# Vision tower, first routing: sets of constant products on TensorE, and three banks for the weights' turns

## The reference

```python
pooled = x.reshape(B, C, 14, 16, 14, 16).sum(axis=(3, 5))      # 16 x 16 patches
h = einsum('bcij,ce->bije', pooled, channel_weights)            # 196 tokens of 192
h = h + attention(layernorm(h), Wq, bq, Wk, bk, Wv, bv)         # one head of 192
# mixture of nested experts on y = layernorm(h)
logits = einsum('bnc,ec->bne', y, w_router); probs = softmax(logits)
gate, idx = top_k(swapaxes(probs, 1, 2), 98)                    # 98 of 196 tokens for each of 4 experts
hidden = w1 on the chosen tokens, the first 24, 48, 96 or 192 features by expert
x_mlp, q, k, v = split(hidden)                                  # 768 and 3 x 192
x_attn = attention with 12 heads of 16 over q, k, v
out = w2 on concat(gelu(x_mlp), x_attn), again by expert, weighted with the gates
h = h + y + both halves of out
```

## Time and profile before

| | us |
|---|---|
| median of 3 runs | 1766.48 |
| lowest, highest | 1763.33, 1769.15 |
| the profiled execution's own time | 1757.22 |
| its span in the profile | 1755.4 |
| TensorE busy | 1517.8 (86%) |
| VectorE busy | 1218.5 (69%) |
| ScalarE busy | 847.3 (48%) |
| mean granted clock of TensorE | 0.939 |

### The profile page before, as it was taken

The page is one execution under the profiler, slowest core; times in us unless marked ns, Lnnn a source line. Parts: engine busy times, 40 slices in busy tenths (PEclk is TensorE's granted clock), DMA queues, the critical chain, the costliest instruction groups (busy, mean ns, idle before and its releaser), DMA issues.

```text
span 1755.4 us, 34644 instructions
## 1 busy us (share of the span) xinstructions
PE 1517.8 (86%) x12440; PEld 1258.9 (72%) x12440; DVE 1218.5 (69%) x2824; ACT 847.3 (48%) x1934; POOL 248.9 (14%) x319
## 2 busy tenths in 40 slices
PE   2146889898998999988998899989899989999998
PEld 2033778687786878777786777778687778878786
DVE  6658678757887578766887488765787677563552
ACT  0002555455554465454554555545554555546653
POOL 3021012200211002200111002300022002110000
PEclk9986889889999899998999899999899999989999
DMA  8985665516662475615673366706655152102220
GB/s 228 241 205 159 164 159 149 144 42 159 170 184 60 110 180 150 163 34 144 162 181 95 86 161 171 187 15 158 145 151 145 38 147 51 35 19 60 50 53 15
DMA packets 99574, 218.02 MB, mean 124 GB/s; under 512 B 61359, under 2 KB 75853, under 8 KB 88654
## 3 DMA queue, kind: packets, MB, share of 16 engines
q10 hardware_dynamic: 12032, 150.94, 32.4%
q1 hardware_dynamic: 87374, 64.88, 16.4%
HBM read 186.57 MB, written 28.90 MB: 123 GB/s over the span
## 4 chain that ended last, share of the span: by engine, by line
PE 50%; DVE 24%; issue 13%; DMA 7%; POOL 3%; ACT 2%; SPq 0%; DVEq 0%; POOLq 0%; ACTq 0%
PE bank L1050 12%; DVE psums L1258 9%; DVE peaks L1458 6%; PE bank L955 6%; PE bank L1019 5%; PE bank L985 5%; PE bank L1004 4%; DMA xt<-in_x_dram 4%; DMA qs<-shiftT 3%; PE bank L967 3%; POOL var L1590 2%; PE bank L878 2%; PE bank L1028 2%; PE bank L829 2%; PE bank L942 2%
## 5 line engine op out<-in xcount | busy, mean ns | idle before, releaser
L1458 DVE TENSOR_REDUCE peaks<-bank 98x2 f32<-98x392 f32 x768 | 423.3, 563 | 173.4 <-PE bank L985 152.7
L1207 ACT ACTIVATE Pb<-bank 98x392 f32<-98x392 f32 x768 | 374.5, 497 | 301.8 <-PE bank L1004 253.3
L1258 DVE TENSOR_REDUCE psums<-xt 112x2 f32<-112x512 f32 x672 | 425.8, 677 | 39.0 <-DMA xt<-in_x_dram 20.8
L1050 PE MATMUL bank<-w2T,hid 128*98 128x192 f32 x1536 | 312.1, 343 | 0.0
L985 PE MATMUL bank<-ks,qs 96*98 96x196 f16 x1536 | 269.3, 262 | 41.8 <-DVE peaks L1458 37.3
L1004 PE MATMUL bank<-qs,ks 97*98 97x196 f16 x1536 | 269.0, 259 | 23.3 <-DMA qs<-shiftT 21.5
L985 PEld LDWEIGHTS bank<-ks,qs 96*98 96x98 f16 x1536 | 166.1, 128 | 132.0 <-DVE peaks L1458 65.2
L1050 PEld LDWEIGHTS bank<-w2T,hid 128*98 128x98 f32 x1536 | 249.9, 176 | 3.6
L1004 PEld LDWEIGHTS bank<-qs,ks 97*98 97x98 f16 x1536 | 167.7, 130 | 35.4 <-DMA qs<-shiftT 24.4
L1019 PE MATMUL bank<-Pb,vals 98*32 98x196 f32 x3072 | 172.6, 343 | 1.2 <-ACT Pb L1207 1.2
L1618 POOL TENSOR_TENSOR fin<-fin,both 98x384 f32<-98x384 f32 x64 | 63.9, 998 | 728.8 <-DVE fin L1483 728.8
(11 more groups left out here) (185 smaller groups left out, 1777.9 us busy)
## 6 DMA issues: line engine op xcount, KB each, us to landing
xt<-in_x_dram ACTq DMA_DIRECT2D x94, 1568.0 KB, 9.0
qk_scratch<-qk SPq DMA_DIRECT2D x64, 294.0 KB, 4.1
qs<-qk_scratch SPq DMA_DIRECT2D x192, 73.5 KB, 3.0
ks<-qk_scratch SPq DMA_DIRECT2D x192, 73.5 KB, 3.1
out_dram<-fin SPq DMA_DIRECT2D x64, 147.0 KB
xt<-in_x_dram SPq DMA_DIRECT2D x2, 1568.0 KB, 15.3
qs<-shiftT SPq DMA_DIRECT2D x128, 2.3 KB
hid<-in_L_ffn_w_dram SPq DMA_DIRECT2D x1, 1440.0 KB
```

The source lines that it names most:

```text
L1050: mm = pe.matmul(misc_ps[slot][0:HT, D * h:D * h + D], lhs, w2T[0:w, f, :], start=(f == 0), stop=(f == NF + 1))
L1207: act.activation(Pb[:, (H * i + h) % NP, :, :].rearrange("p a b -> p (a b)"), score_ps[s][0:HT, 0:2 * T], ACT.Exp, scale=float(DH) ** -0.5 ...
L1258: last = dve.tensor_reduce(psums[:, m % 2, t, 2 * p:2 * p + 2], v[:, 2 * p:2 * p + 2, :, :], AX.XY, ALU.add)
L1458: dve.tensor_reduce(peaks[:, h // 6, :, h % 6], peak_ps[s][0:HT, 0:2 * T].rearrange("p (q k) -> p q k", q=2), AX.X, ALU.max, negate=True). ...
```

## The change

A new operation `warm` on TensorE issues a number of products of `ident` with the first 120 columns of `ident`, f32, into columns 392 to 512 of bank 3, which nobody reads. No other engine takes part in it. Four such sets are put in the list: 50 products just ahead of `norm1_turn`, 36 just ahead of `shift1_turn`, 70 just ahead of `gate_rows`, and 30 just ahead of `chosen`. The last set waits first until ScalarE has copied `M` out of banks 0 to 3; the others wait for nothing. The turns of the weights go round three banks (0 to 2) instead of four: turn n waits for the copy of turn n - 3.

```diff
+WARM = (50, 36, 70, 30)
+LATE_BANKS = 3
+SPARE = (392, 512)
...
+    front += [(slot, ("warm", k, WARM[k])) for k, slot in enumerate((end + 4.4, end + 18.05, at - 1.05, at + 0.5 * ROUNDS + 0.9))]
...
                     for n_ in range(LATE_W1 * part, LATE_W1 if part == 0 else len(late_turns)):
-                        if n_ >= MISC:
-                            pe.wait_ge(late_free, n_ - MISC + 1)
+                        if n_ >= LATE_BANKS:
+                            pe.wait_ge(late_free, n_ - LATE_BANKS + 1)
                         for src, at_, r, w in late_turns[n_][0]:
-                            mm = pe.transpose(banks[n_ % MISC][0:w, at_:at_ + r], src, ident[0:r, 0:r])
+                            mm = pe.transpose(banks[n_ % LATE_BANKS][0:w, at_:at_ + r], src, ident[0:r, 0:r])
                         mm.then_inc(late_full, 1)
...
+            def warm(at, G_, part, n_):
+                if part == 3:
+                    pe.wait_ge(su_act, 2)
+                for k in range(n_):
+                    pe.matmul(peak_ps[1][:, SPARE[0]:SPARE[1]], ident, ident[:, 0:SPARE[1] - SPARE[0]],
+                              start=True, stop=True)
...
-                        act.copy(dst, banks[n_ % MISC][0:parts[0][3], 0:parts[-1][1] + parts[-1][2]]).then_inc(late_free, 1)
+                        act.copy(dst, banks[n_ % LATE_BANKS][0:parts[0][3], 0:parts[-1][1] + parts[-1][2]]).then_inc(late_free, 1)
```

More of the change, by code:

```diff
@@ L1053, in fc2 @@
                     mm.then_inc(misc_full[slot], 1)
-            run(pe, {"fuse": fuse, "planes": planes, "tok": tok, "norm1_turn": norm1_turn, "norm1_key": norm1_key,
+            run(pe, {"warm": warm, "fuse": fuse, "planes": planes, "tok": tok, "norm1_turn": norm1_turn, "norm1_key": norm1_key,
                      "first_max": first_max, "shift1_turn": shift1_turn, "shift1_key": shift1_key,
```

## The result

The changed kernel takes 1782.05 us (median of 4 runs, 1781.67 to 1782.46) where the kernel before takes 1764.9 us (median of 4, 1756.99 to 1769.15). The ratio is 1.0105, with a 95% interval of 1.0071 to 1.0140: slower by 12 to 25 us, 17 by the medians. Forecast were 1780 and +13.6.

A forecast was written before the change was run, and what follows sets the result against it. TensorE, often at half clock, was taken to bound the first routing (about 100 to 190 us) in a chain of waits across engines. 4.9 + 10.5 + 0.2 - 2.0 = +13.6 on the 1766.48 median gave 1780.1 us; range 1767 to 1793.

The forecast's parts named there:

- a product at full clock, at half: Cost of one 120-column f32 product, two records scaled from 196-column ones: 0.203 us at full clock, 0.41 at half.
- `norm1_turn` late by: Behind set 1's 50 products, 10 at half clock and 40 at full: ends at 112.2, so 6.3 us late.
- `shift1_turn` late by: Behind set 2's 36 products at full clock: +4.5 left from set 1 plus 2.9, so +7.4 us.
- left at `first_mix`: Delay left from sets 1 and 2 after faster turn, key and `first_exp` images give time back: +4.9 us.
- rows copied, of that set 3: VectorE's copy of rows before the choosing: set 3's 70 products add +10.5 us, bringing the sum to +15.4.
- set 4: Ahead of `chosen`: M, its copies and 30 products at full clock take 15.7 us against 15.5, so +0.2.
- given back until the first peaks: After `chosen`, turns of u, the first projection and turns run sooner or faster at full clock: gain 2.0 us.
- the last turn of weights waits for a copy behind the exponentials: Ahead of set 3: turn 9 can't start before 150.85, so set 3 begins at 151.3, after over 3 us idle.
- the clock's worth: Time given back by full clock: 1.8 us at the first maxima, 2.5 at shifts and `first_exp`, 2.0 after choosing.
- Rival A: All sets: a product costs what the waits hold, 0.116 us, about one record; +0.1, 1766.6 us; chance 0.11.
- B: All sets hidden by products under 0.08 us, only the clock's gifts of 6.3 us left: 1760.2; chance 0.05.
- C: Building M pulls the clock down, so set 4 costs +9.9 us in place of 0.2: 1789.8; chance 0.17.

The follow-up runs named there:

- e1: The changed kernel with no products, only the turns of weights round three banks; 1758.73 us against 1753.29 for the kernel before, ratio 1.0028.
- e2: The changed kernel with all 186 products, `fuse` part 1 moved ahead of the gates' logits; ratio to the kernel before 1.0112.
- e4: The changed kernel with only the third set (70 products), three banks; ratio to the kernel before 1.0065.
- e7: The changed kernel with sets cut to 18, 18, 34 and 20 products and `fuse` part 1 moved; 1753.74 us against 1760.18 before, ratio 0.9960.
- e6: The changed kernel with all four sets, each product 64 columns wide instead of 120; 1809.15 us, ratio to the kernel before 1.0292.
- e5: The changed kernel with only the fourth set (30 products), three banks; ratio to the kernel before 1.0024.
- e8: The changed kernel with only sets 1 and 2, 18 products each, `fuse` not moved; ratio to the kernel before 0.9937.
- e12: Sets 1 and 2 of 18 products, no later sets, small sets of 2 and 5 in the short waits; 1751.24 us against 1757.66 before, ratio 0.9963.
- e9: The changed kernel with sets of 18, 18 and 34 products, no fourth, `fuse` part 1 moved; ratio to the kernel before 0.9964.

## Why the prediction was right

The prediction was right: slower, by the mechanism that it named. That 1782 and 1780 lie 2 us apart is luck in part, as the marks show step by step, in us:

| step | forecast | measured |
|---|---|---|
| a product at full clock, at half | 0.203, 0.41 us | 0.2235, 0.427 us |
| `norm1_turn` late by | 6.3 | 6.8 |
| `shift1_turn` late by | 7.4 | 8.4 |
| left at `first_mix` | +4.9 | +6.0 |
| rows copied, of that set 3 | +15.4, 10.5 | +18.0, 12.0 |
| set 4 | +0.2 | +2.8 |
| given back until the first peaks | 2.0 | 0.6 |
| sum | +13.6 | +20.2 |

**Right.** That no set fits its wait, that the clock rises within the first set (104.24 to 107.2 by the pace of the records, 2.9 us for a forecast of 4; in the six other profiles that begin with 120 columns it took 4.2 to 5.7), that the last turn of weights waits for a copy behind the exponentials and so takes half of the third wait away (e1, e2), that M at full clock gives nothing (e4), and that the clock's worth is some microseconds at most (e7: 4.1 at `first_mix`, 4.3 forecast as 1.8 and 2.5). Rival A falls by the two records of each product; B with it. C's price didn't come in the changed kernel, where M had 1.00 throughout. Its mechanism is not disproved: with M begun at full clock the clock fell before M was done in e4 (176.20) and in e7 (0.52 in 150.00 to 151.00), some 7 us into it.

**Mis-sized.** First, the pace. I scaled the columns, 0.102 us a record; measured are (8.19 - 0.27)/71 = 0.112. e6 shows that the columns don't matter there. The Trainium skill ("TensorE: Matmul & The Clock Gate", the section on LDWEIGHTS) prices a load by its columns, by an estimate from its formula 107 ns for 128, nearer than my term, and the forecast had set it aside at 1.5 us. The pace at full clock (0.112) is near it; at half clock it is 0.213, twice the page's figure. Over some 140 products at full clock in sets 1 to 3 the 0.02 us make 2.8 us. Second, set 4: I had it start at full clock. At the end of the 1.85 us in which TensorE waited for the copies of M the clock fell, it was down for the first 3.3 us of the set, and the set cost 2.8. Third, the gain after it: the clock was down again in most of 201 to 210 us (0.62), and 0.6 us came instead of 2.0.

The profiled execution was 24.4 us longer in span: 4.2 lie ahead of `tok`, 20.2 between `tok` and the first peaks, and nothing behind (1564 us in both). The timed difference is 17 us, with an interval that holds 20.2. That my 13.6 lies nearer to the 17 is no merit of its terms.

The Trainium skill (same page, Part 1) says that activity releases the throttle, and makes no difference there between kinds of matmul. The traces differ from that: 29.3 us of narrow products (e6) and 15.5 us of M (e5) ran at 0.50 throughout.

## What to carry to other kernels

Work put in to keep TensorE's clock up has to end before the step behind it is ready: the engine does its list in order, and each product over the wait delays all that stands behind it. Count its records and take their pace at both clocks from rows of the same shape, and look for other waits that now share the gap, as the three banks did. Ask first whether the faster stretch is covered by another engine: of four waits, only the two ahead of short dependent chains were worth filling, with 36 to 50 products (e8, e12) instead of 186. Where a program's time scatters by 1%, compare profiles from a common mark just ahead of the change.

## What the runs showed that was not expected

Unbroken work doesn't always raise the clock. M alone (15.47 us busy of 15.50) and f32 products of 64 columns (29.3 of 29.3) stayed at 0.50. In all fourteen sets of 120 columns that began at half clock it rose, by the pace of the records 1.9 to 6.3 us into the set, so one profile doesn't tell when. M begun at 1.00 kept it to its end in three profiles (the changed kernel, e2, e9) and lost it after some 7 us in two (e4, e7).

An f32 product of 128 x 128 weights goes at 0.112 us a record at full clock and 0.213 at half, with 120 columns and with 64.

The start of the kernel scatters. The last tokens' products began at 90.4 to 103.6 us in thirteen further profiles and at 99.3 in before, with nothing changed ahead of them; the time from the first peaks to the end lay between 1557 and 1573 us. Both together are about as large as the effect that was measured.
